# Scores and turned weights of the first attention in single PSUM banks, and orders planned from other durations

## The reference, cut to what matters

```python
x = x + attn_a(layernorm(x))              # stage a: 8 heads of 64, keys and values from a latent of rank 64
x = x + ffn_stack(layernorm(x))           # stages f, f: per depth local attention (window 128) and a gated MLP
x = x + attn_b(layernorm(x))              # stage b: 16 heads of 16, score = dot^2 / |q - k|^2, causal
x = x + ffn_stack(layernorm(x))           # stages f, f

# attn_a, per sequence
q = x @ Wq.T; lat = x @ Wkv_down.T; k = lat @ Wk_up.T; v = lat @ Wv_up.T
out = softmax(q @ k.T / 8) @ v            # full 512 x 512 per head
return out @ Wo.T
```

## Time and profile before

| | |
|---|---|
| median of 3 runs | 4717.62 us (4715.44 to 4721.88) |
| the profiled execution | 4717.21 us |
| its span, first to last instruction | 4715.3 us |
| instructions | 65711 |
| busy: PE, DVE, ACT, POOL | 89%, 71%, 54%, 34% |
| mean granted TensorE clock | 0.948 of full speed |

### The profile page before, as it was taken

One profiled execution on the slowest core, in us unless ns is written; L12 is line 12 of the kernel. 1 busy time (PEld: TensorE's weight loads), 2 busy tenths in 40 slices (PEclk: granted clock), 3 DMA queues, 4 the chain that ended last, 5 costly groups with the idle time before them and its releaser, 6 DMA issues.

```text
span 4715.3 us, 65711 instructions
## 1 busy us (share of the span) xinstructions
PE 4207.5 (89%) x23120; PEld 2616.4 (55%) x23120; DVE 3324.7 (71%) x7849; ACT 2555.6 (54%) x5482; POOL 1603.4 (34%) x1816
## 2 busy tenths in 40 slices
PE   7888888999999999988888878888999999999997
PEld 4545455655655655655555455554565665665654
DVE  5555566676676676648899999988677666667662
ACT  4444444444444444437888888876444444444441
POOL 2122235454454554430000010012554454454441
PEclk9999999999999999997888898888999999999998
DMA  2000000000001000000000000100000000000000
GB/s 72 10 5 15 18 5 12 3 5 3 21 10 28 7 10 12 18 17 19 21 21 21 17 26 21 32 19 18 19 3 5 3 22 10 28 16 19 12 19 20
DMA packets 63094, 78.31 MB, mean 17 GB/s; under 512 B 15344, under 2 KB 47520, under 8 KB 62768
## 3 DMA queue, kind: packets, MB, share of 16 engines
q1 hardware_dynamic: 62768, 74.12, 5.5%
HBM read 36.37 MB, written 12.58 MB: 10 GB/s over the span
## 4 chain that ended last, share of the span: by engine, by line
PE 67%; DVE 19%; ACT 6%; issue 5%; POOL 2%; DMA 0%; SPq 0%; POOLq 0%; DVEq 0%; ACTq 0%
PE wide L782 48%; PE o_ps L782 8%; PE turn_ps L785 6%; PE wide L785 4%; DVE x L1213 3%; DVE w_up L1326 2%; DVE prob L1338 2%; DVE x L1332 2%; PE turn_ps L782 1%; DVE w_up L1311 1%; POOL prob L1542 1%; DVE hid L1332 1%; DVE resid L1398 1%; DVE x L1430 1%; DVE k_t L1273 1%
## 5 line engine op out<-in xcount | busy, mean ns | idle before, releaser
L782 PE MATMUL wide<-x,w_up 128*128 128x512 f32 (+5 forms) x2560 | 864.4, 549 | 27.8 <-DVE x L1430 20.6
L782 PE MATMUL wide<-w_in,x_t 128*128 128x512 f32 (+2 forms) x1920 | 818.0, 570 | 57.1 <-ACT turned L1076 43.8
L1542 POOL TENSOR_SCALAR prob<-prob,st 128x256 f32<-128x256 f32 (+1 forms) x1024 | 449.3, 459 | 989.2 <-DVE st L1362 988.7
L1145 ACT ACTIVATE prob<-prob,st 128x256 f32<-128x256 f32 (+1 forms) x1024 | 479.4, 472 | 315.6 <-DVE st L1349 315.6
L782 PEld LDWEIGHTS wide<-w_in,x_t 128*128 128x128 f32 x1920 | 344.1, 193 | 411.1 <-issue 403.5
L782 PEld LDWEIGHTS wide<-x,w_up 128*128 128x128 f32 (+2 forms) x2560 | 370.9, 195 | 297.9 <-issue 253.1
L782 PE MATMUL o_ps<-pt,v 128*32 128x128 f32 (+2 forms) x5120 | 508.8, 345 | 26.6 <-DVE pt L1375 10.2
L785 PE MATMUL turn_ps<-ident,prob 128*128 128x128 f32 x2480 | 407.4, 283 | 93.5 <-issue 40.3
L1515 POOL TENSOR_TENSOR sines<-raw,rot 128x512 f32<-128x512 f32 x256 | 352.4, 1397 | 334.8 <-ACT raw L1073 334.8
L785 PEld LDWEIGHTS turn_ps<-ident,prob 128*128 128x128 f32 x2480 | 285.2, 142 | 319.5 <-issue 247.5
L1523 POOL TENSOR_TENSOR rn<-ss,minus_half 128x16 f32<-128x16 f32 x128 | 410.0, 3203 | 151.8 <-DVE ss L1259 145.0
(11 more groups left out here) (139 smaller groups left out, 7362.1 us busy)
## 6 DMA issues: line engine op xcount, KB each, us to landing
kept<-resid SPq DMA_DIRECT2D x16, 512.0 KB, 2.6
x<-kept SPq DMA_DIRECT2D x16, 512.0 KB, 3.3
w_up<-hid SPq DMA_DIRECT2D x64, 128.0 KB, 2.2
x<-hid SPq DMA_DIRECT2D x64, 128.0 KB, 2.4
shifted<-resid SPq DMA_DIRECT2D x32, 224.0 KB
w_in<-in_f_wqkv SPq DMA_DIRECT2D x4, 1536.0 KB, 6.9
w_up<-in_f_w SPq DMA_DIRECT2D x4, 1492.0 KB, 7.5
resid<-in_x SPq DMA_DIRECT2D x8, 512.0 KB, 8.6
```

The source lines that it names most:

```text
L782: return eng.matmul(out, lhsT, rhs, start=start, stop=stop, skip_group_check=True)
L1145: last = eng.activation(pr[:, local_span(t)], pr[:, local_span(t)], ACT.Exp, bias=sm[:, t:t + 1], scale=-1.0, accum_out=sm[:, 4 + t:5 + t])
L1542: last = eng.tensor_scalar(pr[:, local_span(t)], pr[:, local_span(t)], sm[:, 8 + t:9 + t], 1.0, ALU.mult, ALU.mult)
```

## The change

1. In stage a, scores are computed and read tile by tile: one score part is one head and one tile in one bank. A pair of score parts is two matmuls. "low" and "exp" become one instruction of 512 columns each per part; `tile_part` numbers the parts, and "inv" follows the second tile.
2. PSUM is planned as seven banks (`BANKS`) beside `o_ps`. `rooms` says which a part may take: in stage a, score, turn_a and turn_b take any single one of five banks (the old `turn_ps` and the four banks of `wide1` and `wide2`), and all other parts take the one pair `wide0` (`A_PAIRS = 1`). In f and b the rooms are as before. `readers_of` no longer lets a score of stage f hold its banks until "exp", which in f reads `prob` in SBUF; `psum_read` waited for "low" alone there already. A part may now have more than one earlier holder to wait for.
3. The durations in `cost` and `B_COST` are replaced for nearly all kinds of all stages. Some waits are dropped from the planner's lists where another implies them.

```diff
+A_PAIRS = 1
...
+def tile_part(k, t):
+
+    return k // 2 * 4 + 2 * t + k % 2
...
-B_COST = {"bclip": (0.3, 0.27), "bnum": (0.1, 0.23), "bguess": (0.2, 0.48), "bclose": (0.1, 0.27), "bmul": (0.5, 0.53),
-          "exp": (0.85, 0.24), "mix": (0.05, 0.33)}
+B_COST = {"bclip": (0.2, 0.255), "bnum": (0.1, 0.21), "bguess": (0.15, 0.475), "bclose": (0.1, 0.277), "bmul": (0.45, 0.525),
+          "exp": (0.64, 0.24), "mix": (0.05, 0.305)}
...
-        return {"score": {"a": 1.92, "f": 1.72}, "mix": {"a": 2.4, "f": 1.68}}[kind][st] if i % 2 else 0.0
+        return {"score": {"a": 1.05, "f": 1.77}, "mix": {"a": 1.85, "f": 1.65}}[kind][st] if i % 2 else 0.0
...
-        "low": {"a": 1.22, "f": 1.87}, "exp": {"a": 1.78, "f": 2.65}, "inv": {"a": 0.68, "f": 0.17},
-        "wt": {"a": 0.98, "f": 2.08}, "turn_a": {"a": 0.62, "f": 0.5}, "turn_b": {"a": 0.62, "f": 0.42},
-        "pt_a": {"a": 0.6, "f": 0.6}, "pt_b": {"a": 0.69, "f": 0.55}}
+        "low": {"a": 0.6, "f": 1.25}, "exp": {"a": 0.7, "f": 1.96}, "inv": {"a": 0.68, "f": 0.15},
+        "wt": {"a": 0.97, "f": 1.75}, "turn_a": {"a": 0.6, "f": 0.5}, "turn_b": {"a": 0.6, "f": 0.42},
+        "pt_a": {"a": 0.59, "f": 0.57}, "pt_b": {"a": 0.65, "f": 0.5}}
...
-        return {"up_g": 1.78, "gate": 0.75}[kind]
-    flat = {"xt": 0.95, "qk": 3.7, "vv": 3.7, "spread": 0.93, "aq": 3.7, "lat": 2.9, "fold_q": 2.5, "fold_o": 2.5, "fold_q_c": 1.03, "fold_o_c": 1.23, "bqkv": 3.7,
-            "bk": 0.65, "bq": 0.65, "proj": 1.72, "xt2": 1.06, "up_g": 3.55, "up_h": 3.55, "down": 2.6, "sel": 2.55, "fan": 0.65,
-            "xt_c": 1.2, "raw": 2.04, "v_c": 1.03, "q_c": 0.6, "aq_c": 1.03, "av_c": 0.4, "bsq": 0.93,
-            "bk_c": 0.57, "bq_c": 0.57, "out": 0.6, "olog": 1.2, "out_b": 0.65, "osum": 1.2,
-            "gelu": 5.6, "bn_h": 2.3, "nrm_h": 1.5, "cos": 2.08, "ss": 1.62, "join": 2.63, "k_c": 0.68, "ak_c": 0.65,
-            "row": 0.95, "bss": 0.8, "res": 1.23,
-            "bn_f": 1.11, "bn_f2": 1.79, "nrm_f": 2.9, "xt2_c": 1.6, "gate": 1.49, "hid": 1.49, "res2": 1.23,
-            "rstd_h": 1.02, "sin": 3.14, "rn": 3.05, "brow": 1.8, "bias_b": 2.4,
+        return {"up_g": 1.78, "gate": 0.7}[kind]
+    if kind == "down":
+        return 2.9 if i % 2 else 2.3
+    flat = {"xt": 0.95, "qk": 3.7, "vv": 3.7, "spread": 0.93, "aq": 3.6, "lat": 2.9, "fold_q": 2.5, "fold_o": 2.5, "fold_q_c": 1.03, "fold_o_c": 1.23, "bqkv": 3.3,
+            "bk": 0.65, "bq": 0.62, "proj": 1.72, "xt2": 1.0, "up_g": 3.55, "up_h": 3.55, "down": 2.85, "sel": 2.5, "fan": 0.62,
+            "xt_c": 1.12, "raw": 1.9, "v_c": 1.0, "q_c": 0.57, "aq_c": 0.95, "av_c": 0.4, "bsq": 0.82,
+            "bk_c": 0.5, "bq_c": 0.5, "out": 0.53, "olog": 1.12, "out_b": 0.62, "osum": 1.2,
+            "gelu": 5.6, "bn_h": 1.9, "nrm_h": 1.4, "cos": 1.25, "ss": 1.65, "join": 2.8, "k_c": 0.6, "ak_c": 0.65,
+            "row": 0.85, "bss": 0.65, "res": 1.2,
+            "bn_f": 0.85, "bn_f2": 1.35, "nrm_f": 3.5, "xt2_c": 1.4, "gate": 1.38, "hid": 1.35, "res2": 1.2,
+            "rstd_h": 1.02, "sin": 2.75, "rn": 3.2, "brow": 1.35, "bias_b": 2.4,
...
-            else:
-                put("score", k, at, final("aq_c", 1), final("ak_c"))
-            put("low", k, at, final("score", k | 1), *scaled, *(turned if st == "f" else []))
+                put("low", k, at, final("score", k | 1), *scaled, *turned)
+            elif k % 2:
+                for t in range(2):
+                    for step in (k - 1, k):
+                        i = tile_part(step, t)
+                        freed = [(kind, *BEFORE[u, step][of]) for kind, of in
+                                 (("wt", "st"), ("turn_a", "prob"), ("turn_b", "prob")) if BEFORE[u, step][of]]
+                        put("score", i, at, final("aq_c", 1), final("ak_c"))
+                        put("low", i, at, final("score", i | 1), *freed[:1])
+                        put("exp", i, at + 1 / steps, final("low", i), *freed[1:])
...
-        put("exp", k, at + 1 / steps, final("bmul" if st == "b" else "low", k), *turned)
+        if st != "a":
+            put("exp", k, at + 1 / steps, final("bmul" if st == "b" else "low", k), *turned)
...
+BANKS = 7
+
+
+def rooms(part):
+
+
+    kind, u, i = part
+    st = stage_of(u)
+    pairs, single = [(f"wide{k}", (2 * k, 2 * k + 1)) for k in range(3)], (f"bank{BANKS - 1}", (BANKS - 1,))
+    if st == "a" and kind in ("score", "turn_a", "turn_b"):
+        return [single] + [(f"bank{k}", (k,)) for k in range(A_PAIRS * 2, BANKS - 1)]
+    if kind in NARROW and not (kind == "turn_a" and st == "b"):
+        return [single]
+    return pairs[:A_PAIRS] if st == "a" else pairs
+
+
+def readers_of(part):
+
+    kind, u, i = part
+    last = [(r, u, 0 if kind in ("proj", "down") else i) for r in READERS[kind]]
+    if kind == "turn_a" and stage_of(u) == "b":
+        last.append(("pt_b", u, i))
+    if kind == "score" and stage_of(u) == "f":
+        last.remove(("exp", u, i))
+    return last
...
-        ring = "narrow" if kind in NARROW and not (kind == "turn_a" and stage_of(u) == "b") else "wide"
         best = None
-        for k, holder in enumerate(rings[ring]):
+        for name, banks in rooms(part):
             at = 0.0
-            if holder is not None:
-                hk, hu, hi = holder
-                last = [(r, hu, 0 if hk in ("proj", "down") else hi) for r in READERS[hk]]
-                if hk == "turn_a" and stage_of(hu) == "b":
-                    last.append(("pt_b", hu, hi))
-                last = [r for r in last if r in parts]
-                if any(r not in end for r in last):
-                    continue
-                at = max(end[r] for r in last) + HOP
-            if best is None or at < best[0]:
-                best = (at, f"{ring}{k}")
+            for holder in {holders[k] for k in banks} - {None}:
+                for r in readers_of(holder):
+                    if r in parts:
+                        at = max(at, end[r] + HOP) if at is not None and r in end else None
+            if at is not None and (best is None or at < best[0]):
+                best = (at, name)
...
-            ring, k = where.rstrip("0123456789"), int(where[-1])
             if holder_of(part) == part:
-                before[part] = rings[ring][k]
-                rings[ring][k] = part
+                banks = dict(rooms(part))[where]
+                before[part] = [h for h in dict.fromkeys(holders[k] for k in banks) if h]
+                for k in banks:
+                    holders[k] = part
...
+        buffers = dict(wide)
+        for k in range(BANKS - 1):
+            buffers[f"bank{k}"] = wide[f"wide{k // 2}"][:, k % 2 * 512:k % 2 * 512 + 512]
+        buffers[f"bank{BANKS - 1}"] = turn_ps
...
-                if HELD.get(part):
-                    psum_read(pe, HELD[part])
+                ps = buffers.get(PLACE.get(part))
+                for held in HELD.get(part, ()):
+                    psum_read(pe, held)
...
-                    pair, half = i // 4, i // 2 % 2
-                    for k in range(2):
-                        t = 2 * half + k
-                        for j in (0, 1):
-                            r = slice(64 * j, 64 * j + 64)
-                            last = mm(wide[PLACE["score", u, i - 1 + j]][:, k * 512:(k + 1) * 512],
-                                      q_t[s][r, pair, t * P:(t + 1) * P], k_t[s][r, 0, :], True, True)
-                            if k == 1:
-                                last.then_inc(S["score"], 1)
+                    pair, t = i // 8, i // 2 % 4
+                    for j in (0, 1):
+                        r = slice(64 * j, 64 * j + 64)
+                        mm(buffers[PLACE["score", u, i - 1 + j]][:, :], q_t[s][r, pair, t * P:(t + 1) * P], k_t[s][r, 0, :],
+                           True, True).then_inc(S["score"], 1)
...
-                    pr, sm = prob[SLOTS[u, i]["prob"]], st[SLOTS[u, i]["st"]]
-                    ps = wide[PLACE["score", u, i]]
+                    step, t = i // 4 * 2 + i % 2, i // 2 % 2
+                    pr, sm = prob[SLOTS[u, step]["prob"]], st[SLOTS[u, step]["st"]]
                     exp_tables()
                     act.wait_ge(S["low"], low_count(u, i))
-                    prob_free(act, u, i)
-                    for k in range(2):
-                        cut = slice(k * 512, k * 512 + 512)
-                        last = eng.activation(pr[:, cut], ps[:, cut], ACT.Exp, bias=sm[:, k:k + 1],
-                                              accum_out=sm[:, 2 + k:3 + k])
-                    last.then_inc(S["exp"], 1)
+                    prob_free(act, u, step)
+                    eng.activation(pr[:, t * 512:t * 512 + 512], buffers[PLACE["score", u, i]][:, :], ACT.Exp,
+                                   bias=sm[:, t:t + 1], accum_out=sm[:, 2 + t:3 + t]).then_inc(S["exp"], 1)
...
-                    st_free(dve, u, i)
```

(27 more changed lines are left out.)

7 lines of the change are left out of this document (3 added, 4 removed).

## The result

The changed kernel takes 4489.12 us (median of 4, 4486.44 to 4495.55), the kernel before 4717.35. The ratio is 0.9517, 95% interval 0.9500 to 0.9533: 228 us less, where 83 were forecast and the range ended at 4570. The sign was right, the size far too small.

The account below looks back on a forecast made before the run. The prediction took TensorE to bound the first stage, with gaps from transposes waiting for one bank. From 4717.2 us it took 56 (banks), 6 (clock), 15 (feed-forward) and 5 (second attention): 4635 us, range 4570 to 4697.

Parts of the forecast that it names:

- the count of bank-us: First stage: scores and transposes need 17.6 of 31 bank-us per pair of steps, 57% of five banks.
- I take the feed-forward's 4.4 us as what stays per sequence: First stage: 4.4 us of waits stay in each of 8 sequences, so 56 of 91.1 us are gained.
- 6 us forecast for the clock: First stage: some busy time comes back as the granted clock rises, 6 us within bounds 0 and 26.
- I take a quarter, -15 us: Feed-forward stages: earlier end of hold and new durations give -15 us, bounds -64 and +64.
- 5 beside the quarter above: Second attention: new durations fit queue occupancy better, value -5 us, bounds +40 and -60.
- is planned as long as before: Feed-forward normalisation: planned chain 5.7 us against 5.8, so its wait, 24.5 us in 13 sequences, should stay.
- a hop is planned 0.1 us too early: All stages: new durations follow queue occupancy, so cross-engine waits are planned about 0.1 us too early.
- A: Later stages: orders gain too, 64 us in feed-forward and 24 in second attention; 4567 us, chance 13%.
- B: First stage: one projection pair binds or the score chain comes late, 41 of 56 us not gained; 4676 us, 12%.
- D: First stage: finer gaps lower the granted clock to 0.85, +25 us; 4742 us, chance 2%.
- E: First stage: waits move from transposes to scores, later stages keep their length; 4710 to 4725 us, chance 5%.
- C: Feed-forward: evictions planned too early cost 3 us more per sequence; 4751 us, chance 6%.

Follow-up runs that it names:

- e6: Changed kernel with two pairs kept for projections, so first-stage scores and transposes share three single banks instead of five: 4623.21 us, ratio 0.9784.
- e3: Kernel before with one planner edit: a feed-forward score holds its banks until the maximum, not the exponential: 4639.17 us, ratio 0.9828.
- e7: Changed kernel with the planned nrm_f duration at the measured 4.7 us instead of 3.5: 4455.77 us, ratio 0.9423.
- e2: Kernel before with the new durations alone (first stage keeps old ones for score, low, exp), old banks and hold: 4695.15 us, ratio 0.9945.
- e11: e7 with the planned hop between engines at 0.3 us instead of 0.2 everywhere: 4626.41 us, ratio 0.9797.
- e5: Kernel before, but first-stage transposes may take turn_ps or any free two-bank room; scores whole, old durations and hold: 4785.22 us, ratio 1.0122.
- e9: e5 with the new durations of e2: 4733.3 us, ratio 1.0026.
- e12: Changed kernel with first-stage transposes in turn_ps alone; scores, split by tile, take the four banks of the two other rooms: 4541.02 us, ratio 0.9606.

## Why the prediction was wrong

**Right.** What bounded the stage, and the mechanism: four groups of transposes per pair, two waiting for one bank. The maximum of 512 columns takes 0.680 us (0.69 forecast), hidden on VectorE (its groups by form, 150 to 600 us):

```profile
L1389 DVE TENSOR_REDUCE st<-wide 128x1 f32<-128x512 f32 x161 | 102.8, 680 | 6.1 <-PE wide L823 3.2 <-PE turn_ps L823 2.0
```

The one pair of rooms for the projections costs little: two groups of projections wait 3.2 and 2.1 us up to 609.5 us, where they waited 0.0 and 0.2. Five banks are enough and three are not, as the count of bank-us had it (e6). Its shares, 57% and 94%, hold for a stretch in which a pair of steps takes 6.25 us; over a whole sequence of 67.2 us the same 8 x 17.6 bank-us are 42% of five banks and 70% of three.

**The first step that failed: "I take the feed-forward's 4.4 us as what stays per sequence".** 1.0 us stayed in a sequence inside the stage. The nearest row was of a stage bound by TensorE, but its waits were not a floor of such stages: they had causes of their own, a false hold (e3) and a duration of 2.9 us for 4.74 (e7), and with both mended that stage too has 0.5% idle. The upper bound in the text, all of the 91 us, was nearer: 87 us of the waits before these transposes went. Other waits took 13 back, so 74 us of idle time went where 56 were forecast.

**A term of the same stage was mis-sized too: busy time, 6 us forecast for the clock, 28 measured.** About 13 of them are 66.18 us for the work of 67.84 at the same clock of 1.00, eight times; the prediction had no term for it. The other 14 or so, by difference, go with the clock, 0.98 before and 1.00 now. 74 and 28 make the 102 us.

**The second, and by far the larger: "I take a quarter, -15 us" for the hold and the durations, with -64 as what the bank waits could give.** The four feed-forward stages gave 110 us. The hold alone gives 81 us, on top of the banks 89. "On TensorE, busy 95%, an earlier bank is worth no more than its waits" is what broke, in two ways. A true room changes the order, and with it the wait for the normalisation (19.0 to 12.5 us in 10 sequences in e3), which hangs on no bank. And busy time shrinks with the waits (84.1 to 83.2 us per sequence in e3), which no row of waits shows. Even all 4.4 us of waits is no upper bound: of the 4.0 us per sequence that the changed kernel gained, 3.0 are gaps and 1.0 is busy time, and e7 gained 5.1.

**The durations** gave 36 us, where the forecast had 5 beside the quarter above. The argument that nrm_f "is planned as long as before" and its wait "should stay" fell: the durations alone bring it from 19.0 to 10.3 us in 10 sequences (e2), and e7 shows that what was left came from the planned 3.5 us. That a hop is planned 0.1 us too early can cost no more than the small waits that e7 has left (4.1 us in 900); planning it later everywhere (e11) made the kernel 3.7% slower.

**The rivals.** A was the nearest (4567 us for the later stages' gain) and had part of the mechanism, the feed-forward's bank waits; it still priced the first stage as the forecast did. B, D and E did not happen: stage a's clock is 1.00 while its results go round five banks. The Trainium skill ("TensorE: Matmul & The Clock Gate", section "A second HAM failure mode: psum-queue depth-cycling") describes cycling through banks with frequent short idles between groups; this trace doesn't show the clock switching there, and the stage has 1.5% of idle time. What D feared did happen in other orders of the same work: e2, e5 and e9 have 0.92 to 0.94. C did not happen in the change, but the danger was real and larger than its 3 us per sequence: e11 has 6 more than e7.

**Open.** Why the same correction of nrm_f gains 0.9% on the new durations and loses 0.4% on the old ones, beyond that the order is another one. How the 36 us divide among some sixty durations was not tried. Nor was it tried which of the new durations gives e2's first stage the order that has the lower clock. How the clock's share and the shorter busy time divide the 28 us is a difference, not a run.

## What to carry to other kernels

Idle time that a planned order leaves in front of one engine is no floor of the stage: look for the false statement in the planner (a reader that doesn't read, a duration well under the measured one), since both found here cost more than the wait they were seen at, and let the range reach the whole wait and beyond, as TensorE's busy time shrinks too. Count rooms as time held against time available, over the shortest stretch in which they are all used: 57% left almost no waits, 94% brought them back. Read a lost microsecond as idle or busy before giving it a cause: in e2 the gaps stayed and the clock had changed. A greedy order answers a small change of one number by percents in either direction, so every correction has to be run, and a gain has to be read per stage.

## What the runs showed of the hardware that was not expected

**Beginning a group costs busy time, gap or no gap.** The same 398 matmuls of a sequence have 66.18 us of busy time in the changed kernel, 67.84 before and 69.05 in e12, all at a clock of 1.00. Gaps don't explain it: they are 1.0, 11.6 and 4.4 us. The number of groups goes with it. Counting in TensorE's timeline each place where the kind of work changes (transposes, scores, mixes, projections) or where a gap interrupts one kind, a sequence has 38, 52 and 60 of them; an estimate from the differences is 0.12 to 0.13 us each. It is no constant: the first sequence of e6, also at 1.00, has 70.7 us with 51 of them, above what this estimate gives; 23 of its groups begin behind a gap, 14 or fewer in the other three. In the first row below, 16 transposes follow each other and the next kind starts 1.89 us later, 0.47 per four; in e12 (third and fourth row) four stand alone and the next kind starts 0.59 us later.

```profile
223.43 1.97 PE L826 MATMUL wide<-ident,prob 128*128 128x128 f32 x16
225.32 0.69 PE L823 MATMUL turn_ps<-k_t,q_t 64*128 64x512 f32 x1
```

```profile
389.59 0.66 PE L826 MATMUL turn_ps<-ident,prob 128*128 128x128 f32 x4
390.18 1.95 PE L823 MATMUL o_ps<-pt,v 128*64 128x256 f32 x16
```

So five banks gave more than room to wait less: they let transposes come in longer runs. What in the engine takes the time is not shown, and the ends of matmuls in a profile are modelled; the distances between starts are not.

**The share of idle time in a sequence does not settle the clock.** The drop to 0.96 in a sequence with 14% of gaps was gone at 1.5%; in e12, with 6% of TensorE idle between 300 and 600 us, the clock is 1.00 as well, and in e6, with 13% between 200 and 500 us, 0.97. But the other sequence of the earlier trace rows has nearly the same share of gaps at 1.00, and e2, with 13%, has 0.92. Windows of 4 us in e2 (PE first) show what the engine did: in one place it was busy 1.25 of 4 us and the clock fell to 0.58 in the next window, mostly the lower of its two levels, 1.2 GHz; in another it was busy 2.48 of 4 us and the clock stayed. Which form of gaps brings the lower level was not isolated.

```profile
236.00:240.00 4.00, 1.25 (x10) 0.81 (x9) 2.73 (x6) 3.59 (x10) 1.59 (x2) 1.00 0.00 0
240.00:244.00 4.00, 4.00 (x13) 1.48 (x12) 0.80 (x2) 0.00 (x0) 0.38 (x1) 0.58 0.02 6
256.00:260.00 4.00, 2.48 (x15) 1.41 (x15) 2.61 (x6) 2.34 (x6) 1.82 (x2) 1.00 0.00 0
260.00:264.00 4.00, 4.00 (x30) 2.09 (x26) 2.36 (x2) 2.27 (x6) 0.00 (x0) 1.00 0.01 2
```
